# Mixing the running maxima and minima of two graph convolutions on ScalarE and VectorE instead of TensorE

## The chip, the cores and the metric

The kernel runs on one core of one Trainium2 chip. The metric is the device time of one execution in microseconds. TensorE multiplies, VectorE and ScalarE work elementwise, GpSimd issues the indirect DMAs (gathers and scatters by index), and SyncE issues most of the plain loads and fills. The engines run side by side, each through its own list of instructions in order, and wait for each other at semaphores.

## The reference

Eight graph layers run one after the other on the same 100,000 nodes of 128 features and 50,000 edges sorted by target: three GCN layers, two "eve" layers (`L1`), two SAGE layers and one attention layer. The change concerns the two eve layers alone. Cut to what matters, one of them is:

```
def eve_conv(x, src, dst, wpool, bpool, wself, weve, wconv, bconv, bias):
    p = relu(x @ wpool.T + bpool)
    m = p[src]
    xmax = segment_max(m, dst, num_segments=n)      # 0 where a node has no edge
    xmin = segment_min(m, dst, num_segments=n)
    eve = relu(wconv[0] * xmax + wconv[1] * xmin + bconv[0])
    return x @ wself.T + eve @ weve.T + bias

h = eve_conv(feat, ..., wpool1, ...); h = relu(h); h = eve_conv(h, ..., wpool2, ...)
x = layernorm(x + h)
```

`wconv` is two numbers and `bconv` one.

## The kernel before

Each layer is a phase of its own (`Conv`), called m4 and m5 for the two eve layers; a phase ends with a barrier of all engines. In a phase the edges are taken in 49 chunks of 1024 and the nodes in 49 pairs of chunks of 1024. On each engine `merged_sweep` writes the order: a unit of edge work (a pair of chunks, that is four halves of 512 edges), then the node pairs that the finished edges make ready (three each after the third and the fourth unit, two after each later one), then the next unit. There are 24 units of four halves and one of two, so 98 halves in a phase.

GpSimd (`pool_program`) has a list of its own: for each chunk eight gathers of 128 source rows into `rows` (L1073) and, four or five chunks behind, eight scatters of `result` into the table `sums` (L1081), with a copy of the indices (L1060) between. A scatter waits for `e_out_read`, which the last step of its half on VectorE raises.

A half `i` of the edge work (`EveEdges`) passes through these steps:

- TensorE turns the gathered rows into `e_turn` (L1122), of which there is one bank.
- ScalarE copies it to `xT` (L1486) and makes `begin` from the run flags (L1493).
- TensorE multiplies `xT` with the pooling weight into one of two banks named `pool` (L1435).
- ScalarE adds the bias and takes the relu in place (L1499).
- VectorE scans the bank twice, for the running maximum `hi` (L1531) and the running minimum `lo` (L1535).
- TensorE multiplies `hi` and `lo` with two diagonal matrices, the identity times `wconv[0]` and times `wconv[1]`, and sums both products into the same bank (L1442, L1443, function `mix`).
- ScalarE adds `bconv` and takes the relu into the SBUF tile `mix` (L1480).
- TensorE multiplies `mix` with `weve` into `e_out`, one bank (L1132).
- VectorE adds the bias into `result` (L1518).

On TensorE the order in half `i` is: mix of `i-1`, turn of `i+1`, multiply of `i-1`, pool of `i+1`. The mix and the product of a unit's last half therefore stand at the head of the next unit, behind the node pairs. The diagonal matrices (`k["mix1"]`, `k["mix2"]`) are made once in `load_constants` (L249).

The node work (`LinearNodes`) turns and multiplies a pair of node chunks on TensorE (L1190, L1208, in m5 also L1204 for a residual input), with `nodeT` on ScalarE (L1223), the sum `z` on VectorE (L1775) and the output `o` on ScalarE. In m4 this is one relu per chunk (L1811). In m5 it is a layer norm, with statistics on VectorE (L712), a root on ScalarE (L753) and sixteen scaled copies on ScalarE (L759).

Of the kernel before, what the change touches and what calls it, by code (L numbers as in the profile page):

```python
# [24 lines left out]
ALU = mybir.AluOpType  # L25
# [134 lines left out]
def load_constants(nc, a, k):  # L160
# [20 lines left out]
    with Phase(nc, "const") as ph:  # L181
# [14 lines left out]
        mix_made = ph.sem("mix_made")  # L196
# [8 lines left out]
        with nc.Block() as block:  # L205
# [38 lines left out]
            def _(dve):  # L244
                dve.wait_ge(loaded, 16 * len(loads))
                dve.wait_ge(ident_made, 1)
                for i in (1, 2):
                    for m in range(2):
                        dve.tensor_scalar(k[f"mix{i}"][:, m, :], k["ident"][:, :], k[f"wconv{i}"][:, m:m + 1], None, ALU.mult).then_inc(mix_made, 1)  # L249
                dve.wait_ge(mix_made, 4)  # L250
# [1156 lines left out]
class EveEdges:  # L1407


    def __init__(self, ph, no):  # L1410
# [3 lines left out]
        self.mix_w, self.bconv, self.bias = k[f"mix{no}"], k[f"bconv{no}"], k[f"eve_r{no}"]  # L1414
# [5 lines left out]
        self.mixed, self.mix_relu = ph.sem("mixed"), ph.sem("mix_relu")  # L1420
# [7 lines left out]
    def tensor(self, pe, j, par, q, halves, back):  # L1428
        ph = self.ph

        def pool(i):
            g = 4 * j + i
            pe.wait_ge(ph.e_turn_read, g + 1)
            wait_from(pe, self.mix_relu, g - 1)
            pe.matmul(self.bank[i % 2][:, :], self.wpool[:, :], self.xT[:, i % 2, :], start=True, stop=True).then_inc(self.pooled_ps, 1)  # L1435

        def mix(jj, i):

            g = 4 * jj + i
            pe.wait_ge(self.hi_done, g + 1)  # L1440
            pe.wait_ge(self.lo_done, g + 1)
            pe.matmul(self.bank[i % 2][:, :], self.mix_w[:, 0, :], self.hi[:, i % 2, :], start=True, stop=False)  # L1442
            pe.matmul(self.bank[i % 2][:, :], self.mix_w[:, 1, :], self.lo[:, i % 2, :], start=False, stop=True).then_inc(self.mixed, 1)  # L1443
# [14 lines left out]
        for i in range(halves):  # L1458
            before_half(mix, i)
# [9 lines left out]
        if halves == 0:  # L1469
            before_half(mix, 0)  # L1470
            before_half(multiply, 0)

    def scalar(self, act, j, par, q, halves, back):
        ph = self.ph

        def relu(jj, i):
            g = 4 * jj + i
            act.wait_ge(self.mixed, g + 1)
            wait_from(act, ph.e_multiplied, g - 3)
            act.activation(self.mix[:, i, :], self.bank[i % 2][:, :], ACT.Relu, bias=self.bconv[:, 0:1]).then_inc(self.mix_relu, 1)  # L1480
# [20 lines left out]
        for i in range(halves):  # L1501
# [5 lines left out]
            if i:  # L1507
                relu(j, i - 1)
        if halves == 0 and back:
            relu(j - 1, back - 1)  # L1510

    def vector(self, dve, j, par, q, halves, back):
# [13 lines left out]
        def scans(i):  # L1526
            g = 4 * j + i
            dve.wait_ge(self.pooled, g + 1)
            start = scan_start(dve, self.hi_done, self.hi, g, i)
            wait_from(dve, self.mixed, g - 1)  # L1530
# [6 lines left out]

        for i in range(halves):
            scans(i)
            result_before(i)  # L1540
# [1043 lines left out]
def build(nc, a, out):  # L2584
# [17 lines left out]
    with ExitStack() as ctx:  # L2602
# [29 lines left out]
        for n in ("mix1", "mix2"):  # L2632
            keep(n, [P, 2, D], stack=early)
# [46 lines left out]
```

## Time and profile before

| what | us |
|---|---|
| median of 3 runs (10847.68 to 10850.53) | 10850.13 |
| the profiled execution, its own time | 10843.73 |
| its span | 10841.9 |
| m4 (first eve layer), in the span | 4604 to 5627 |
| m5 (second eve layer) | 5627 to 6815 |

Busy shares over the whole span are 66% for GpSimd, 62% for TensorE, 57% for VectorE and 42% for ScalarE, but each layer has its own limit, so they are read by layer. In a view of stretches "PEclk" is the granted TensorE clock as a share of full speed. In a timeline a row gives the start, the duration, the engine, the line, what is written from what, and in brackets how long the engine had been idle and who released it. "issue" means that nothing the profile shows was waited for.

### The profile page before, as it was taken

What the parts mean: (1) busy time and instruction counts of PE and PEld (TensorE: products, weight loads), DVE (VectorE), ACT (ScalarE), POOL (GpSimd) and SP (SyncE); (2) the same over time, 40 slices, a digit from 0 to 9 for tenths busy, and PEclk for the clock granted to TensorE, in tenths of its full rate; (3) what the DMA queues carried; (4) which work ended last, traced back from release to release, by engine and by line L of the source; (5) the groups of instructions that cost most, each with busy time, mean ns of one, the idle gap of its engine ahead of it and who ended that gap; (6) DMA issues with size and microseconds to landing.
All of it is one profiled execution on the core that took longest, in us unless ns stands there. A gap on an engine that the chain in (4) does not pass through costs nothing. (4 is left out here: it accounts for less than half of the span.)

```text
span 10841.9 us, 165885 instructions
## 1 busy us (share of the span) xinstructions
PE 6744.0 (62%) x36946; PEld 5118.8 (47%) x36947; DVE 6202.3 (57%) x16059; ACT 4581.5 (42%) x8583; POOL 7208.8 (66%) x7532
## 2 busy tenths in 40 slices
PE   2005766677667669978767888445467656555552
PEld 2004666566656653355545555444455543333331
DVE  5225666566556656544435555333355547888888
ACT  0111222233223325544435555333345545777777
POOL 5736776777677750077767665677677767777772
PEclk9998888788889889988989999777778877777775
DMA  7887887799889978767768777677688863433333
GB/s 190 184 200 240 281 281 250 263 344 319 283 284 337 328 266 283 265 217 258 253 209 281 259 267 260 215 247 251 235 276 313 297 221 98 126 127 126 125 119 105
DMA packets 1864966, 2570.80 MB, mean 237 GB/s; under 512 B 255901, under 2 KB 1369141, under 8 KB 1864662
## 3 DMA queue, kind: packets, MB, share of 16 engines
q1 hardware_dynamic: 1134168, 1627.20, 45.5%
q10 hardware_dynamic: 504726, 564.87, 15.5%
q0 software_dynamic: 225792, 375.94, 10.9%
q14 instruction: 220, 1.80, 0.1%
q8 instruction: 60, 0.98, 0.0%
HBM read 1499.55 MB, written 1129.98 MB: 243 GB/s over the span
## 5 line engine op out<-in xcount | busy, mean ns | idle before, releaser
L1081 POOL DMA_INDIRECT sums_gcn<-m_result,m_idx x1176 | 1166.9, 992 | 430.9 <-issue 349.1
L1190 PE MATMUL m_n_bank<-k_ident,m_in_y 128*128 128x128 f32 x5488 | 848.1, 312 | 891.8 <-DMA m_in_y<-node_rows_c 381.0
L1073 POOL DMA_INDIRECT m_rows<-node_rows_a,m_idx x1176 | 1127.7, 959 | 339.6 <-issue 335.8
L1223 ACT ACTIVATE m_nodeT<-m_n_bank 128x512 f32<-128x512 f32 x980 | 535.6, 597 | 1725.7 <-PE m_n_bank L1190 1723.4
L1775 DVE TENSOR_TENSOR m_z<-m_n_bank,m_in_sums 128x512 f32<-128x512 f32 (+1 forms) x784 | 505.7, 686 | 1306.6 <-ACT m_o L1811 355.0
L1190 PEld LDWEIGHTS m_n_bank<-k_ident,m_in_y 128*128 128x128 f32 x5488 | 719.3, 162 | 983.7 <-issue 791.4
L1081 POOL DMA_INDIRECT sums_eve<-m_result,m_idx x784 | 766.0, 977 | 407.4 <-issue 230.1
L1081 POOL DMA_INDIRECT sums_sage<-m_result,m_idx x784 | 765.9, 977 | 268.4 <-issue 231.4
L1686 DVE SCALAR_TENSOR_TENSOR m_acc<-m_n_bank,m_scales,m_res_b 128x128 f32<-128x128 f32 (+1 forms) x2352 | 634.2, 342 | 487.7 <-PE m_n_bank L1208 421.0
L1073 POOL DMA_INDIRECT m_rows<-node_rows_b,m_idx x784 | 754.4, 962 | 226.4 <-issue 222.1
L1629 PE MATMUL m_gram<-m_y 128*128 128x129 f32 (+1 forms) x4800 | 689.5, 308 | 340.6 <-ACT m_y L1655 339.3
L1629 PEld LDWEIGHTS m_gram<-m_y 128*128 128x128 f32 (+1 forms) x4800 | 652.2, 220 | 374.8 <-ACT m_y L1655 372.9
L1122 PE MATMUL m_e_turn<-k_ident,m_rows 128*128 128x128 f32 x2744 | 512.0, 320 | 499.1 <-DVE m_sums L1585 183.6
L1122 PEld LDWEIGHTS m_e_turn<-k_ident,m_rows 128*128 128x128 f32 x2744 | 391.4, 166 | 637.5 <-DVE m_sums L1585 187.1
L759 ACT ACTIVATE m_o<-m_z,m_ln_shift,m_ln_scale 128x128 f32<-128x128 f32 x1600 | 628.4, 485 | 94.6 <-DMA node_rows_c<-m_o 45.0
L1060 POOL COPY m_idx<-k_edge_idx 128x16 int32 (+1 forms) x350 | 74.6, 215 | 872.5 <-POOLq L106 871.8
L2203 POOL DMA_INDIRECT sums_gat<-g_result,g_idx x392 | 453.3, 1156 | 294.3 <-DVE g_result L2497 179.7
L1208 PE MATMUL m_n_bank<-k_gcn,m_nodeT 128*128 128x128 f32 (+1 forms) x4704 | 589.6, 280 | 0.0
L1132 PE MATMUL m_e_out<-k_gcn,m_sums 128*128 128x128 f32 x2352 | 409.4, 329 | 286.7 <-DVE m_result L1402 286.7
L1931 POOL DMA_INDIRECT degree<-deg_both_tab,k_edge_idx x392 | 456.4, 1164 | 179.0 <-issue 119.2
L1208 PEld LDWEIGHTS m_n_bank<-k_gcn,m_nodeT 128*128 128x128 f32 (+1 forms) x4704 | 567.4, 197 | 0.0
L1132 PEld LDWEIGHTS m_e_out<-k_gcn,m_sums 128*128 128x128 f32 x2352 | 357.3, 232 | 346.4 <-DVE m_result L1402 180.9
(299 smaller groups left out, 17513.2 us busy)
## 6 DMA issues: line engine op xcount, KB each, us to landing
m_in_sums<-sums_gcn SPq DMA_DIRECT2D x291, 512.0 KB
m_in_y<-node_rows_a SPq DMA_DIRECT2D x291, 512.0 KB
sums_gcn<-k_gcn_b SPq DMA_DIRECT2D x194, 512.0 KB
node_rows_a<-m_y ACTq DMA_DIRECT2D x194, 512.0 KB
m_in_x<-in_x_dram SPq DMA_DIRECT2D x194, 512.0 KB
m_in_y<-node_rows_b SPq DMA_DIRECT2D x194, 512.0 KB
sums_eve<-k_eve_b SPq DMA_DIRECT2D x194, 512.0 KB
m_in_sums<-sums_eve SPq DMA_DIRECT2D x194, 512.0 KB
```

Of the source, the lines that this page charges most:

```text
L759: ins = act.activation(out[0:n, j, :], z[0:n, j, :], ACT.Identity, bias=self.shift[copy][0:n, at:at + 1], scale=self.scale[copy][0:n, at:a ...
L1073: pool.indirect_dma_start(self.rows[b][:, t, :], None, self.table[:, :], bass.IndirectOffsetOnAxis(self.idx[s][:, t:t + 1], 0)).then_inc(s ...
L1081: pool.indirect_dma_start(self.node_sums[:, :], bass.IndirectOffsetOnAxis(self.idx[s][:, T + t:T + t + 1], 0), self.result[b][:, t, :], No ...
L1122: mm = pe.transpose(bank[:, n * P:(n + 1) * P], self.rows[b][:, H * (i % 2) + n, 0:D], self.k["ident"][:, :])
L1132: mm = pe.matmul(bank[:, n * D:(n + 1) * D], lhs[:, n * P:(n + 1) * P], weight[:, :], start=True, stop=True)
L1190: mm = pe.transpose(self.n_bank[i][:, t * P:t * P + n], self.buf["y"][i // 2][0:n, H * (i % 2) + t, :], self.k["ident"][0:n, 0:n])
L1208: mm = pe.matmul(self.n_bank[i][0:n, t * D:(t + 1) * D], self.nodeT[:, i, t * P:t * P + n], weight[:, :], start=not add, stop=not add or t ...
L1223: act.activation(out, src, ACT.Copy).then_inc(self.n_turn_read, 1)
L1629: mm = pe.matmul(self.gram[:, 0:D + 1], self.y1[b][0:rows[b], t, 0:D], self.y1[b][0:rows[b], t, :], start=False, stop=False, skip_group_ch ...
L1686: ins = dve.scalar_tensor_tensor(out=self.acc[b][0:n, tt, :], in0=ph.node_out(i, n)[:, t, :], scalar=self.scales[b][0:n, tt:tt + 1], in1=s ...
L1775: dve.tensor_tensor(self.z[b][0:n, half, :], ph.node_out(i, n), ph.buf["sums"][b][0:n, half, :], ALU.add).then_inc(ph.n_out_read, 1)
L1931: pool.indirect_dma_start(self.dram["degree"][:, :], bass.IndirectOffsetOnAxis(k["edge_idx"][:, c, 1, t:t + 1], 0), self.both_tab[:, c * T ...
```

## The change

TensorE no longer mixes. After the scan of the maxima, ScalarE writes `wconv[0] * hi + bconv` into `mix` (new step `scale_hi`, an Identity with a scale and a bias). After the scan of the minima, VectorE adds `wconv[1] * lo` to it in place (new step `mix`, one instruction with `lo` and `mix`, both in SBUF, as inputs). ScalarE then takes the relu of `mix` in place. The diagonal matrices and the four instructions that made them are gone. The bank `pool` is free for the next product when the scan of the minima is done (`lo_done`), and no longer when the relu is. The line numbers of the change are lower than those of before by 5 to 9 here.

```
         def pool(i):
             pe.wait_ge(ph.e_turn_read, g + 1)
-            wait_from(pe, self.mix_relu, g - 1)
+            wait_from(pe, self.lo_done, g - 1)
             pe.matmul(self.bank[i % 2], self.wpool, self.xT[:, i % 2, :])
-        def mix(jj, i):
-            pe.wait_ge(self.hi_done, g + 1)
-            pe.wait_ge(self.lo_done, g + 1)
-            pe.matmul(self.bank[i % 2], self.mix_w[:, 0, :], self.hi[:, i % 2, :], start=True, stop=False)
-            pe.matmul(self.bank[i % 2], self.mix_w[:, 1, :], self.lo[:, i % 2, :], start=False, stop=True)
...
         def relu(jj, i):                                   # ScalarE
             act.wait_ge(self.mixed, g + 1)
-            wait_from(act, ph.e_multiplied, g - 3)
-            act.activation(self.mix[:, i, :], self.bank[i % 2], ACT.Relu, bias=self.bconv)
+            act.activation(self.mix[:, i, :], self.mix[:, i, :], ACT.Relu)
+        def scale_hi(i):
+            act.wait_ge(self.hi_done, g + 1)
+            wait_from(act, ph.e_multiplied, g - 3)
+            act.activation(self.mix[:, i, :], self.hi[:, i % 2, :], ACT.Identity, bias=self.bconv, scale=self.wconv[:, 0:1])
...
             pool(i)
             if i:
                 relu(j, i - 1)
+            scale_hi(i)
...
+        def mix(i):                                        # VectorE
+            dve.wait_ge(self.hi_scaled, g + 1)
+            dve.wait_ge(self.lo_done, g + 1)
+            dve.scalar_tensor_tensor(out=self.mix[:, i, :], in0=self.lo[:, i % 2, :], scalar=self.wconv[:, 1:2],
+                                     in1=self.mix[:, i, :], op0=ALU.mult, op1=ALU.add)
         for i in range(halves):
             scans(i)
+            mix(i)
             result_before(i)
```

ScalarE in the third half of a unit, before (the first row is the relu of an earlier half, the others are the copy, `begin` and the pooling relu of the next one):

```order
L1480 ACTIVATE m_mix<-m_pool,k_bconv 128x512
L1484 REGISTER_ALU
L1486 ACTIVATE m_xT<-m_e_turn 128x512
L1493 REGISTER_ALU
L1493 ACTIVATE m_begin<-k_same_run 128x512
L1499 ACTIVATE m_pool<-m_pool,k_bpool 128x512
```

And at the same place in the change:

```order
L1464 ACTIVATE m_mix<-m_mix 128x512
L994 REGISTER_ALU
L1470 ACTIVATE m_mix<-m_hi,k_bconv,k_wconv 128x512
L1475 REGISTER_ALU
L1477 ACTIVATE m_xT<-m_e_turn 128x512
L1484 REGISTER_ALU
L1484 ACTIVATE m_begin<-k_same_run 128x512
L1490 ACTIVATE m_pool<-m_pool,k_bpool 128x512
```

The scaling of `hi` now stands between the relu and the copy of the next half.

VectorE in the same half, before:

```order
L1531 SCALAR_TENSOR_TENSOR m_hi<-k_same_run,m_hi,m_pool 128x512
L1535 SCALAR_TENSOR_TENSOR m_lo<-m_begin,m_lo,m_pool 128x512
L1518 TENSOR_TENSOR m_result<-m_e_out,k_eve_r 128x512
L1528 REGISTER_ALU
L1531 REGISTER_ALU
```

And in the change:

```order
L1524 SCALAR_TENSOR_TENSOR m_hi<-k_same_run,m_hi,m_pool 128x512
L1528 SCALAR_TENSOR_TENSOR m_lo<-m_begin,m_lo,m_pool 128x512
L1535 SCALAR_TENSOR_TENSOR m_mix<-m_lo,k_wconv,m_mix 128x512
L1510 TENSOR_TENSOR m_result<-m_e_out,k_eve_r 128x512
L1520 REGISTER_ALU
L1524 REGISTER_ALU
```

The addition stands behind the two scans and ahead of the previous half's result. (The first two rows are the scans; the trace names them TENSOR_TENSOR_SCAN.)

## Rows read from the trace of the kernel before

**Rows 1.** Stretches: start:end, length, busy us of each engine, PEclk, DMA share.

```profile
core 0: us, PE busy (x) PEld busy (x) DVE busy (x) ACT busy (x) POOL busy (x), PEclk, DMA share, GB/s
4604.00:5627.00 1023.00, 772.21 (x4116) 543.01 (x4116) 431.59 (x492) 439.11 (x688) 766.79 (x834) 0.90 0.73 243
5627.00:6815.00 1188.00, 935.87 (x4508) 605.94 (x4508) 646.79 (x1627) 659.65 (x1438) 766.83 (x834) 0.92 0.74 252
...
5720.00:6740.00 1020.00, 833.40 (x4040) 542.82 (x4040) 573.25 (x1469) 585.67 (x1281) 680.43 (x737) 0.93 0.78 270
6950.00:7700.00 750.00, 375.88 (x2719) 360.94 (x2720) 267.85 (x541) 258.91 (x304) 575.64 (x625) 0.76 0.74 260
7900.00:8800.00 900.00, 632.85 (x3573) 509.54 (x3574) 513.73 (x1669) 513.88 (x1042) 690.49 (x749) 0.82 0.87 306
```

**Rows 2.** Waits of GpSimd in m4, then in m5: total us, times, longest.

```profile
POOL sums_eve L1081 <- DVE m_result L1518: 7.2, 1, 7.2
...
POOL sums_eve L1081 <- DVE m_result L1518: 167.7, 22, 23.8
```

**Rows 3.** Groups by line, 5720 to 6740: busy us, mean ns, idle before.

```profile
L1442 PE MATMUL m_pool<-m_hi,k_mix 128*128 128x512 f32 x170 | 97.5, 658 | 14.7 <-DVE m_lo L1535 14.7
L1443 PE MATMUL m_pool<-m_lo,k_mix 128*128 128x512 f32 x170 | 90.0, 612 | 0.0
```

**Rows 4.** Timeline of one unit of m5, three engines.

```profile
5861.71 1.28 DVE L1531 TENSOR_TENSOR_SCAN m_hi<-k_same_run,m_hi,m_pool 128x512 f32<-128x512 f32 x1 [1.67 <-ACT m_pool L1499]
...
5864.66 1.27 DVE L1531 TENSOR_TENSOR_SCAN m_hi<-k_same_run,m_hi,m_pool 128x512 f32<-128x512 f32 x1
...
5869.96 1.28 DVE L1531 TENSOR_TENSOR_SCAN m_hi<-k_same_run,m_hi,m_pool 128x512 f32<-128x512 f32 x1 [0.95 <-ACT m_pool L1499]
...
5871.56 0.59 ACT L1486 ACTIVATE m_xT<-m_e_turn 128x512 f32<-128x512 f32 x1
5871.72 1.16 PE L1132 MATMUL m_e_out<-k_eve,m_mix 128*128 128x128 f32 x8 [0.42 <-ACT m_mix L1480]
5872.04 0.63 ACT L1493 ACTIVATE m_begin<-k_same_run 128x512 f32 x1
5872.71 1.02 PE L1435 MATMUL m_pool<-m_xT,k_pool 128*128 128x512 f32 x2
5873.57 1.02 PE L1442 MATMUL m_pool<-m_hi,k_mix 128*128 128x512 f32 x2
5873.77 0.66 ACT L1499 ACTIVATE m_pool<-m_pool,k_bpool 128x512 f32<-128x512 f32 x1 [1.10 <-PE m_pool L1435]
5874.43 1.02 PE L1443 MATMUL m_pool<-m_lo,k_mix 128*128 128x512 f32 x2
5874.56 1.28 DVE L1531 TENSOR_TENSOR_SCAN m_hi<-k_same_run,m_hi,m_pool 128x512 f32<-128x512 f32 x1 [0.95 <-ACT m_pool L1499]
5876.23 1.16 PE L1132 MATMUL m_e_out<-k_eve,m_mix 128*128 128x128 f32 x8 [0.78 <-ACT m_mix L1480]
```

**Rows 5.** The attention layer's timeline, VectorE and GpSimd; then two groups of the page.

```profile
9068.14 0.75 DVE L2476 SCALAR_TENSOR_TENSOR g_prob<-g_val,k_blb,g_prob 128x512 f32<-128x512 f32 x1
9068.93 1.28 DVE L2479 TENSOR_TENSOR_SCAN g_num<-g_fall,g_num,g_prob 128x512 f32<-128x512 f32 x1
...
9069.19 1.80 POOL L2203 DMA_INDIRECT sums_gat<-g_result,g_idx  x1 [0.30 <-issue]
...
L1081 POOL DMA_INDIRECT sums_eve<-m_result,m_idx x784 | 766.0, 977 | 407.4 <-issue 230.1
...
L2203 POOL DMA_INDIRECT sums_gat<-g_result,g_idx x392 | 453.3, 1156 | 294.3 <-DVE g_result L2497 179.7
```

**Rows 6.** Timeline of m5 from node work into the next unit.

```profile
5899.13 1.02 PE L1443 MATMUL m_pool<-m_lo,k_mix 128*128 128x512 f32 x2
...
5903.23 0.69 ACT L1480 ACTIVATE m_mix<-m_pool,k_bconv 128x512 f32<-128x512 f32 x1 [2.22 <-issue]
...
5905.76 1.91 PE L1435 MATMUL m_pool<-m_xT,k_pool 128*128 128x512 f32 x2
```

**Rows 7.** Timeline of VectorE in the constants phase.

```profile
32.57 0.87 DVE L249 TENSOR_SCALAR k_mix<-k_ident,k_wconv 128x128 f32<-128x128 f32 x4 [32.45 <-DMA k_bconv<-in_L_gnn_bconv_dram]
```

More of the change, by code:

```diff
@@ L246, in _ @@
                 dve.wait_ge(ident_made, 1)
[L247 to L250, printed above, removed]
                 for i, n in enumerate(turned):
@@ L1413, in __init__ @@
         self.wpool, self.weve, self.bpool = k[f"pool{no}"], k[f"eve{no}"], k[f"bpool{no}"]
-        self.mix_w, self.bconv, self.bias = k[f"mix{no}"], k[f"bconv{no}"], k[f"eve_r{no}"]
+        self.wconv, self.bconv, self.bias = k[f"wconv{no}"], k[f"bconv{no}"], k[f"eve_r{no}"]
         self.xT, self.begin, self.hi, self.lo = (ph.sb(n, [P, 2, HALF]) for n in ("xT", "begin", "hi", "lo"))
@@ L1419, in __init__ @@
         self.hi_done, self.lo_done = ph.sem("hi_done"), ph.sem("lo_done")
-        self.mixed, self.mix_relu = ph.sem("mixed"), ph.sem("mix_relu")
+        self.hi_scaled, self.mixed, self.mix_relu = ph.sem("hi_scaled"), ph.sem("mixed"), ph.sem("mix_relu")
     def sync(self, sp, j, par, q, halves, back):
@@ L1458, in tensor @@
         for i in range(halves):
-            before_half(mix, i)
             if i + 1 < halves and i:
@@ L1469, in tensor @@
         if halves == 0:
-            before_half(mix, 0)
             before_half(multiply, 0)
@@ L1478, in relu @@
             act.wait_ge(self.mixed, g + 1)
+            act.activation(self.mix[:, i, :], self.mix[:, i, :], ACT.Relu).then_inc(self.mix_relu, 1)
+        def scale_hi(i):
+            g = 4 * j + i
+            act.wait_ge(self.hi_done, g + 1)
             wait_from(act, ph.e_multiplied, g - 3)
-            act.activation(self.mix[:, i, :], self.bank[i % 2][:, :], ACT.Relu, bias=self.bconv[:, 0:1]).then_inc(self.mix_relu, 1)
+            act.activation(self.mix[:, i, :], self.hi[:, i % 2, :], ACT.Identity, bias=self.bconv[:, 0:1],
+                           scale=self.wconv[:, 0:1]).then_inc(self.hi_scaled, 1)
         def copy(i):
@@ L1529, in scans @@
             start = scan_start(dve, self.hi_done, self.hi, g, i)
+            wait_from(dve, self.hi_scaled, g - 1)
             wait_from(dve, self.mixed, g - 1)
@@ L1536, in scans @@
                                    ALU.min).then_inc(self.lo_done, 1)
+        def mix(i):
+            g = 4 * j + i
+            dve.wait_ge(self.hi_scaled, g + 1)
+            dve.wait_ge(self.lo_done, g + 1)
+            dve.scalar_tensor_tensor(out=self.mix[:, i, :], in0=self.lo[:, i % 2, :], scalar=self.wconv[:, 1:2], in1=self.mix[:, i, :],
+                                     op0=ALU.mult, op1=ALU.add).then_inc(self.mixed, 1)
         for i in range(halves):
             scans(i)
+            mix(i)
             result_before(i)
```

6 lines of the change are left out of this document (removed).

## The prediction

> **What bounds the kernel now.** I read the stretches of the two layers first, then who waits for whom, then one unit row by row. In m4 (4604 to 5627) GpSimd is busy 767 of 1023 us [rows 1], and the rest is almost all the fixed gap between its indirect DMAs: it waits for a result only once, 7.2 us, at the very end [rows 2]. An indirect DMA takes 0.977 us and the gap 0.30 [rows 5], so 49 chunks of 16 make 784 x 1.277 = 1001 us. The reader should see that m4 is GpSimd's issue time and nothing else: whatever TensorE saves there ends nothing sooner. In m5 GpSimd has the same 784 to issue, but the layer takes 1188 us, and it waits 167.7 us for `m_result` in 22 waits [rows 2]. There the units and the node pairs, in their fixed order on TensorE, ScalarE and VectorE, set the pace, with TensorE busy 833 of 1020 us [rows 1]. A gain can come from m5 alone, and at most about those 167.7 us.
>
> **TensorE's removed work, and what is late next.** The two removed products hold TensorE from 5873.57 to about 5875.29, that is 1.72 us a half at the full clock [rows 4], 187.5 us in the 1020 us of m5 [rows 3]. In the regular rhythm before, starts of the scan of the maxima stand 4.60 us apart (5869.96, 5874.56) [rows 4], and TensorE fills that time with one idle gap of 0.42. After the change the rhythm is another chain, since ScalarE's list has the new scaling behind the scan and ahead of the next copy: scan 1.28 plus 0.05 to ScalarE, scaling until the copy can start 0.55 (not in the trace; the nearest rows are 0.63 for `m_begin` from SBUF and 0.59 for the copy, which overlap their follower by about 0.1), copy 0.59 and 0.05, pooling product until ScalarE starts 1.06 (5872.71 to 5873.77), its relu 0.66 and 0.13 to the scan (5873.77 to 5874.56) [rows 4]. The sum is 4.37 us. VectorE itself needs at most 2 x 1.28 for the scans and 2 x 0.75 for the addition and the result, 4.1 us a half, so it isn't the bound. The first gap of a unit was 2.95 (5861.71 to 5864.66) and the second 5.30 [rows 4]; all three now become 4.37. Three gaps make 13.1 instead of 12.85: **0.25 us lost per unit**. At a unit's end TensorE was done with the product of the third half at 5876.23 + 1.16, or 2.83 after the last scan's start [rows 4]; now the relu of that half needs no mix, starts right behind the pooling relu (5874.43), takes 0.63, and the product ends about 1.65 after the scan's start. The nodes' first turn follows TensorE, so the node pairs start 1.18 us sooner. Net 0.93 us x 24 units = **-22 us in m5**, at the full clock. What must hide there: ScalarE's last scaling ends about 2.0 after the scan's start, before the first turned nodes reach it.
>
> At a unit's start nothing is gained. TensorE had the last half's mix done by 5900.15, but ScalarE, still with the nodes' outputs, came to its relu at 5903.23 [rows 6]. The mix was already hidden, and the same relu is late in the change.
>
> **The clock.** In the 1020 us of m5 TensorE was granted 0.93. Where it is less busy it is granted less: 0.82 at 70% busy and 0.76 at 50% [rows 1]. Without the 187.5 us it would be 63% busy in m5, so I take 0.82. With two levels, 2.4 and 1.2 GHz, the low one holds for 14% of the time before and 36% after. At the low level the pooling product, which is on the new chain, runs 1.91 instead of 1.02 at 5905.76 [rows 6, 4], and ScalarE starts about 1.0 later. 98 halves x 0.22 x 1.0 = **+22 us in m5**. The bounds are 0 (the clock holds) and 45 (a low share of 60% in the edge work). In m4 the same is covered by GpSimd, as long as a pair of units' chain stays under its 41 us a unit.
>
> **The addition and GpSimd.** The new addition reads two tensors in SBUF. No VectorE step of the edge work did so before. What that does is to be seen in the attention layer: a scan with two SBUF inputs runs 1.28 us from 9068.93, to 9070.21, and the scatter that GpSimd began at 9069.19 takes 1.80 us instead of 0.97, ending 0.78 after the scan [rows 5]. Its fixed part behind the hold is thus about 0.77, and the hold lasts from 0.2 after its start to the scan's end. Over that layer a scatter takes 1156 ns against 977 in the eve layers [rows 5]. For an instruction of length L that falls anywhere in GpSimd's rhythm of 1.277, the expected hold is L x L / (2 x 1.277). The addition is not in the trace; the nearest row is the 0.75 of L2476 [rows 5], which gives 0.22 us, and 0.69 would give 0.19. 98 x 0.20 = **+20 us in m4**, where GpSimd is the bound and every hold counts. The bounds are 0 (it never meets) and 98 x 0.5 = 49 (it always meets in the middle). In m5 GpSimd has its waits to swallow it; I take **+5**, between 0 and 20.
>
> The Trainium skill, page "SBUF — State Buffer", section "Who interferes with whom", says that a VectorE instruction with two SBUF inputs contends with a GpSimd instruction that reads SBUF, and that the second to start is blocked for the whole of the first. By that rule the change has this price. The trace agrees, with 1.80 against 0.97 us [rows 5]. The same section of the Trainium skill infers that `tensor_tensor` doesn't hold up descriptor generation, since that needs the write side. By that the price would be nil and the sum 25 us lower, and the row of 1.80 us speaks against it.
>
> **The rest.** The four multiplications for the diagonal matrices, 0.87 us with their wait [rows 7], go; the first weights were turned 0.4 us later than these began, so about **-1**. ScalarE's scaling costs 98 x 0.55 = 54 us of its time per layer; it is in the chain above for m5, and in m4 (439 us busy of 1023 [rows 1]) it is covered. The wait for `hi_scaled` on VectorE ends during the scan of the minima (about 1.28 us, like the other, against 0.05 + 0.63). Behind ScalarE's new wait for `hi_done` stand the copy, `begin` and the pooling relu of the next half, and TensorE and VectorE wait for those: that is the chain counted above.
>
> **The sum.** m4 +20; m5 -22 + 22 + 5 = +5; constants -1; together +24. From the profiled execution's 10843.7 that is 10867.7; the median of the runs stands 6.4 above it, so **10874 us**.
>
> **Rivals.**
> - The clock holds: m5's +22 is nil and the time 10852. For it: the units' regular part keeps TensorE 60% busy in short gaps only. Against: 0.82 at 70% [rows 1].
> - The clock is low in most of the edge work: +45 (98 x 0.46 x 1.0) instead of +22, so 10897. For it: at a unit's start it is low already, and there is less work than before to raise it [rows 6].
> - GpSimd is not held: 25 less, 10849. Against it stands the 1.80 [rows 5].
> - Faster: ScalarE comes to the first relu of a unit sooner than now. If it gains the 3.1 us by which it is late behind TensorE's mix [rows 6], the removed mix at a unit's head counts too: 24 x 1.72 = 41 us more, and GpSimd's waits in m5 shrink with it. Then the time is 10874 - 41 - 5 = 10828 or less. It decides when ScalarE's relu starts within 0.1 us of its mix being there. Against it: ScalarE gets more work, not less.
> - The change doing nothing at all isn't open: the products are gone from TensorE's list.
>
> **How the numbers follow.** The forecast has 0.43, and its own range is 10859 to 10889; the low clock 0.24, the held clock 0.14, GpSimd not held 0.08, faster 0.11. A measurement of this kernel tells about 0.2%, 22 us, from no change, so the limits are 10828 and 10872. The forecast lies on the upper one and gives 0.23 to slower and 0.20 to same; with the low clock slower has 0.47; the held clock, GpSimd not held and 0.01 of the last rival bring same to 0.43; faster has 0.10. The range from 10835 to 10905 leaves out the faster rival and what lies above the low clock's.
>
> **What would show it.** Right: m4 longer by 16 to 24 us, with indirect DMAs of 1.1 to 1.6 us wherever the addition runs, and a mean over all of m4 up by 0.02 to 0.03; m5 within 15 us of its 1188; granted clock near 0.82 in m5; scan starts 4.3 to 4.5 apart at the full clock. Wrong: m4 unchanged (GpSimd isn't held), m5 shorter by over 20 (the clock or the unit's start), or scan starts under 4.2 apart.

## The result, and the profile after

The change makes the kernel slower. Its median is 10903.74 us (10893.25 to 10909.83) against 10847.68 us of the kernel before in the same measurement; the ratio is 1.0055 with a 95% interval of 1.0042 to 1.0069. The forecast was +24 us and it came to +56: above the forecast's own range (10859 to 10889), and only just inside the wide one (up to 10905). The profiled execution has a span of 10905.8 us against 10841.9.

I measure a layer from its first indirect DMA to the first one of the next layer, since GpSimd's list is the same in both kernels.

| stretch | before | after | difference | forecast |
|---|---|---|---|---|
| up to m4's first DMA | 4605.2 | 4603.1 | -2.1 | -1 |
| m4 | 1023.6 | 1038.8 | +15.2 | +20 |
| m5 | 1187.8 | 1242.8 | +55.0 | +5 |
| from m6 to the end | 4025.3 | 4021.0 | -4.3 | 0 |

So m4 came out near what was worked out, and the error is in m5. The stretches of m4, of m5 and of the steady part of m5, in the change (start:end, length, busy us of each engine with instruction counts, PEclk, DMA share, GB/s; compare [rows 1]):

```profile
4603.00:5641.00 1038.00, 669.71 (x3724) 528.07 (x3724) 500.98 (x590) 506.88 (x786) 781.40 (x832) 0.80 0.73 240
5641.00:6884.00 1243.00, 850.10 (x4116) 599.32 (x4116) 715.58 (x1726) 728.92 (x1536) 780.10 (x837) 0.82 0.71 241
5720.00:6790.00 1070.00, 756.36 (x3702) 535.14 (x3702) 630.44 (x1534) 645.97 (x1365) 703.27 (x750) 0.84 0.74 255
```

TensorE lost its 392 mix records in each layer, yet its busy time in m5 fell by only 86 us (935.87 before, 850.10 now), since what is left ran slower: the granted clock fell from 0.92 to 0.82. In m4 GpSimd's busy time rose from 766.79 to 781.40, with the same DMAs.

GpSimd's waits in m4 and then in m5 of the change (us in total, times, longest; compare [rows 2]):

```profile
POOL sums_eve L1076 <- DVE m_result L1510: 8.5, 1, 8.5
...
POOL sums_eve L1076 <- DVE m_result L1510: 208.7, 21, 25.3
```

In m4 it still waits once, at the end. In m5 its waits grew by 41 us; the DMAs themselves are 13 us longer (below), and that is the 54 by which the time from its first to its last DMA grew (1159.0 to 1213.4). m5 is paced by the other engines, as forecast.

**The regular chain.** Two halves of m5 in the change at the full clock (start, duration, engine, line; compare [rows 4]):

```profile
6038.34 1.28 DVE L1524 TENSOR_TENSOR_SCAN m_hi<-k_same_run,m_hi,m_pool 128x512 f32<-128x512 f32 x1 [0.77 <-ACT m_pool L1490]
...
6039.66 0.81 ACT L1470 ACTIVATE m_mix<-m_hi,k_bconv,k_wconv 128x512 f32<-128x512 f32 x1 [0.89 <-DVE m_hi L1524]
...
6040.38 0.58 ACT L1477 ACTIVATE m_xT<-m_e_turn 128x512 f32<-128x512 f32 x1
...
6040.90 0.75 DVE L1535 SCALAR_TENSOR_TENSOR m_mix<-m_lo,k_wconv,m_mix 128x512 f32<-128x512 f32 x1
...
6041.01 1.13 PE L1430 MATMUL m_pool<-m_xT,k_pool 128*128 128x512 f32 x2 [1.03 <-ACT m_xT L1477]
6041.19 1.30 POOL L1076 DMA_INDIRECT sums_eve<-m_result,m_idx  x1 [0.30 <-issue]
...
6042.17 0.66 ACT L1490 ACTIVATE m_pool<-m_pool,k_bpool 128x512 f32<-128x512 f32 x1 [0.70 <-PE m_pool L1430]
...
6042.95 1.28 DVE L1524 TENSOR_TENSOR_SCAN m_hi<-k_same_run,m_hi,m_pool 128x512 f32<-128x512 f32 x1 [0.71 <-ACT m_pool L1490]
```

The chain is the one of the prediction, scan, scaling, copy, product, relu, scan, but 4.61 us long and not 4.37: the copy starts 0.72 behind the scaling and not 0.55, and ScalarE's relu 1.16 behind the product's start and not 1.06, because TensorE now comes to the product from an idle gap (in the kernel before, the product at 5862.06 came from one of 0.83, and there it was 1.17). The row at 6041.19 is a held DMA, one that took longer than its usual 0.97 because VectorE's addition was running: it began 0.29 after the addition's start and took 1.30 instead of 0.97.

**The first gap of a unit.** The same chain where the clock is low:

```profile
6075.69 1.28 DVE L1524 TENSOR_TENSOR_SCAN m_hi<-k_same_run,m_hi,m_pool 128x512 f32<-128x512 f32 x1 [3.39 <-ACT m_pool L1490]
...
6077.08 0.81 ACT L1470 ACTIVATE m_mix<-m_hi,k_bconv,k_wconv 128x512 f32<-128x512 f32 x1 [1.68 <-DVE m_hi L1524]
6077.80 0.58 ACT L1477 ACTIVATE m_xT<-m_e_turn 128x512 f32<-128x512 f32 x1
...
6078.43 2.07 PE L1430 MATMUL m_pool<-m_xT,k_pool 128*128 128x512 f32 x2 [2.87 <-ACT m_xT L1477]
...
6080.54 0.66 ACT L1490 ACTIVATE m_pool<-m_pool,k_bpool 128x512 f32<-128x512 f32 x1 [1.64 <-PE m_pool L1430]
...
6081.32 1.28 DVE L1524 TENSOR_TENSOR_SCAN m_hi<-k_same_run,m_hi,m_pool 128x512 f32<-128x512 f32 x1 [1.72 <-ACT m_pool L1490]
```

TensorE had been idle for 2.87 us and the product takes 2.07 instead of 1.13. Scan to scan is 5.63 us. Of 21 units the three gaps averaged 3.14, 5.67 and 4.59 before and average 5.40, 5.00 and 4.68 now, 15.08 in sum instead of 13.40. From a unit's last scan to the next unit's first one it was 33.87 and is 34.45.

**The end of a unit.** The nodes' first turn, in the kernel before and in the change (TensorE alone):

```profile
6347.10 1.96 PE L1190 MATMUL m_n_bank<-k_ident,m_in_y 128*128 128x128 f32 x16 [0.71 <-issue]
6393.07 1.96 PE L1190 MATMUL m_n_bank<-k_ident,m_in_y 128*128 128x128 f32 x16 [0.83 <-issue]
...
6240.34 3.50 PE L1185 MATMUL m_n_bank<-k_ident,m_in_y 128*128 128x128 f32 x16 [0.82 <-issue]
6387.12 3.50 PE L1185 MATMUL m_n_bank<-k_ident,m_in_y 128*128 128x128 f32 x16 [0.71 <-issue]
```

Between 5870 and 6700 us this turn ran at the full clock, in 1.96 us, at all 18 unit ends before, and in the change at 5 of the 17 whose turn stands in one row; at the other 12 it took 2.43 to 3.51. ScalarE waits for it, and the node pairs behind it. This is the loss that the prediction has no term for.

### The profile page after: what moved, and what is told of

The parts are those of the page before. It is cut to its first block and busy times, and to the rows that moved or that the text cites. A ratio compares the mean times of both kernels' runs of the same rounds, so it can differ in the third digit from the quotient of the medians.

```text
span 10905.8 us, 164896 instructions
## 1 busy us (share of the span) xinstructions
PE 6525.5 (60%) x36162; PEld 5068.9 (46%) x36163; DVE 6332.6 (58%) x16251; ACT 4716.2 (43%) x8779; POOL 7234.6 (66%) x7532
## 5 line engine op out<-in xcount | busy, mean ns | idle before, releaser
L1185 PE MATMUL m_n_bank<-k_ident,m_in_y 128*128 128x128 f32 x5488 | 878.2, 320 | 880.6 <-DMA m_in_y<-node_rows_c 386.2
L1185 PEld LDWEIGHTS m_n_bank<-k_ident,m_in_y 128*128 128x128 f32 x5488 | 748.4, 166 | 973.2 <-issue 771.4
L1117 PE MATMUL m_e_turn<-k_ident,m_rows 128*128 128x128 f32 x2744 | 536.2, 331 | 498.3 <-DVE m_sums L1586 173.5
L1127 PE MATMUL m_e_out<-k_eve,m_mix 128*128 128x128 f32 x1568 | 308.4, 357 | 353.8 <-ACT m_mix L1464 349.3
```

Of the source, the lines that this page charges most:

```text
L1117: mm = pe.transpose(bank[:, n * P:(n + 1) * P], self.rows[b][:, H * (i % 2) + n, 0:D], self.k["ident"][:, :])
L1127: mm = pe.matmul(bank[:, n * D:(n + 1) * D], lhs[:, n * P:(n + 1) * P], weight[:, :], start=True, stop=True)
L1185: mm = pe.transpose(self.n_bank[i][:, t * P:t * P + n], self.buf["y"][i // 2][0:n, H * (i % 2) + t, :], self.k["ident"][0:n, 0:n])
```

## The experiments

Two theories of m5's 55 us. A: ScalarE's order, with the scaling between a scan and the next copy, makes most of it. B: the lower clock makes most of it. A third matter is whether the two SBUF inputs of the addition hold GpSimd. The table has all runs; the ratio is to the kernel before, measured on the same chip, "held" counts the DMAs of a layer that took over 1.05 us. The layer columns come from one profiled execution of each kernel, whose total can stand far from the kernel's median (10898.61 against 10877.00 for extra_add, 10878.77 against 10862.30 for product_and_psum, 10807.53 against 10826.82 for no_scale). What the two layers differ by from before agrees with the difference of the medians within 15 us in each kernel, so differences of 10 us between rows are weak evidence by themselves.

| kernel | ratio (95%) | m4 | m5 | clock m5 | held m4, m5 |
|---|---|---|---|---|---|
| before | 1 | 1023.6 | 1187.8 | 0.92 | 0, 0 |
| change | 1.0055 (1.0042 to 1.0069) | 1038.8 | 1242.8 | 0.82 | 37, 40 |
| only_m5 | 1.0039 (1.0025 to 1.0053) | 1021.9 | 1238.0 | 0.83 | 0, 38 |
| psum_input | 1.0035 (1.0021 to 1.0049) | 1031.1 | 1232.9 | 0.83 | 0, 0 |
| extra_add | 1.0016 (1.0007 to 1.0025) | 1037.5 | 1205.2 | 0.90 | 27, 18 |
| no_scale | 0.9987 (0.9978 to 0.9996) | 1024.1 | 1167.1 | 0.86 | 7, 3 |
| late_scale | 0.9968 (0.9956 to 0.9980) | 1022.8 | 1151.4 | 0.87 | 9, 3 |
| late_first | 1.0029 (1.0019 to 1.0040) | 1030.4 | 1210.0 | 0.82 | 34, 27 |
| late_filler | 1.0008 (0.9999 to 1.0017) | 1032.6 | 1190.7 | 0.85 | 45, 17 |
| extra_product | 1.0019 (1.0010 to 1.0028) | 1035.9 | 1199.7 | 0.90 | 35, 26 |
| product_and_psum | 1.0011 (1.0002 to 1.0020) | 1018.7 | 1208.6 | 0.88 | 0, 0 |
| extra_scale | 1.0088 (1.0075 to 1.0102) | 1056.2 | 1267.8 | 0.89 | 0, 0 |
| late_product | 0.9954 (0.9940 to 0.9968) | 1021.6 | 1130.8 | 0.90 | 6, 4 |

**One layer alone.**

> The change in the second eve layer alone, m4 as before. The two layers don't touch each other: m4 1022 to 1024, m5 1244 as in the change, total 10885 to 10892. If m5 comes out shorter than 1235, part of its loss was carried over from m4 (the state of the clock at its start, or the chip).

It went as expected: m4 as before, m5 within 5 us of the change's. The layers are independent, and 5 us is also how far two profiles of the same m5 stood apart here.

**The addition's inputs.**

```
-            wait_from(pe, self.lo_done, g - 1)
+            wait_from(pe, self.mixed, g - 1)
...
-            dve.scalar_tensor_tensor(out=self.mix[:, i, :], in0=self.lo[:, i % 2, :], ...
+            dve.scalar_tensor_tensor(out=self.mix[:, i, :], in0=self.bank[i % 2][:, :], ...
```

> The addition reads the PSUM bank in place of lo, so that it has one SBUF input (mix) instead of two; the minima are left out of the result. Theory (two SBUF inputs hold GpSimd's indirect DMAs): m4 goes back from 1038 to 1023 to 1026, the mean scatter in it from 996 to about 977 ns, and m5 gains 0 to 5 us; total 10883 to 10890. Rival (m4's 15 us come from the added steps' timing, not from their inputs): m4 stays at 1036 to 1040 and the total at 10900.

GpSimd's groups in m5, first of the change, then of this kernel (busy us, mean ns):

```profile
L1076 POOL DMA_INDIRECT sums_eve<-m_result,m_idx x392 | 389.9, 995 | 322.2 <-DVE m_result L1510 208.7 <-issue 112.6 <-DMA sums_eve<-m_result,m_idx 0.9
L1068 POOL DMA_INDIRECT m_rows<-node_rows_a,m_idx x392 | 379.4, 968 | 113.2 <-issue 112.9 <-PE m_e_turn L1117 0.3
...
L1076 POOL DMA_INDIRECT sums_eve<-m_result,m_idx x392 | 382.5, 976 | 326.5 <-DVE m_result L1510 213.6 <-issue 112.3 <-DMA sums_eve<-m_result,m_idx 0.6
L1068 POOL DMA_INDIRECT m_rows<-node_rows_a,m_idx x392 | 372.8, 951 | 113.1 <-issue 113.1
```

The addition takes as long (751 ns), and with one input in PSUM not one DMA is held. The mechanism is shown. In m4 the DMAs are 14 us shorter in sum (769.4 to 755.1), but only 7.7 of the 15 us came back, so the number expected of m4 was missed. GpSimd's last wait shows why:

```profile
POOL sums_eve L1076 <- DVE m_result L1510: 17.6, 2, 14.7
```

It was 8.5. Behind GpSimd the slowed units of m4 stand close, and took half of what it got back. m5 gained 10.

**The same addition in the kernel before**, its result discarded:

```
             scans(i)
+            dve.wait_ge(self.lo_done, 4 * j + i + 1)
+            dve.scalar_tensor_tensor(out=self.extra, in0=self.lo[:, i % 2, :], scalar=self.wconv[:, 1:2], in1=self.hi[:, i % 2, :],
+                                     op0=ALU.mult, op1=ALU.add)
             result_before(i)
```

> The kernel before, with the same addition of two SBUF tensors on VectorE (0.75 us a half, its result discarded) behind the two scans, in both layers. VectorE has room for it. Theory (a GpSimd DMA that starts inside such an addition is held): 25 to 45 DMAs of each layer take over 1.05 us, none in the kernel before; GpSimd's DMA time in each layer is 8 to 20 us longer; m4 is 5 to 18 us longer and m5 0 to 15 us; the ratio to before 1.001 to 1.003. Rival (the held DMAs come with ScalarE's scaling): no DMA over 1.05 us and no change.

It holds DMAs and brings m4's 14 us with no other part of the change, and 17 in m5, slightly over the bound that I set there. The rival, that ScalarE's scaling holds the DMAs, falls. The 14 and the 17 are not all holds: the DMA time grew by 9.1 us in m4 and 5.7 in m5, the step also lengthens VectorE's list (a unit's first gap is 3.76 instead of 3.14), and this profile is 22 us above its kernel's median. The cleaner figure for m5 is the 10 us of the kernel with one input in PSUM, where the DMA time fell by 14; the forecast had 5.

**The scaling taken away, and the scaling placed late.** In the first kernel:

```
-            act.activation(self.mix[:, i, :], self.mix[:, i, :], ACT.Relu)
+            act.activation(self.mix[:, i, :], self.mix[:, i, :], ACT.Relu, bias=self.bconv, scale=self.wconv[:, 0:1])
...
-            scale_hi(i)
...
-            dve.scalar_tensor_tensor(..., in0=self.lo[:, i % 2, :], scalar=self.wconv[:, 1:2], in1=self.mix[:, i, :], ...
+            dve.scalar_tensor_tensor(..., in0=self.lo[:, i % 2, :], scalar=self.ratio, in1=self.hi[:, i % 2, :], ...
```

> The scaling is gone from ScalarE: the addition is now hi + (w1/w0) * lo, and the relu applies w0 and the bias (w1/w0 is made once among the constants). ScalarE's next copy no longer stands behind the scan of the maxima. Theory A (the scaling between scan and copy made the chain of m5): scan starts in a unit come 4.0 to 4.4 apart at all three gaps, 12.0 to 13.2 instead of 15.1 for three, so 24 units are 45 to 75 us shorter; m5 from 1244 to 1170 to 1200, m4 stays at 1038 because the two-input addition is still there. Total 10830 to 10860. Theory B (the low TensorE clock made m5 longer, whatever the order on ScalarE): m5 stays over 1220 and the total over 10880.

In the second:

```
             copy(i)
             begin(i)
+            if i:
+                scale_hi(i - 1)
             pool(i)
             if i:
                 relu(j, i - 1)
-            scale_hi(i)
+        if halves:
+            scale_hi(halves - 1)
```

> Only the place of the scaling in ScalarE's list is changed: the copy and begin of the next half go ahead of it, and the scaling is still 0.8 us long. Theory A (its place between scan and next copy is what costs): m5 shortens like in the kernel without scaling, by 40 to 70 us, to 1175 to 1205, with scan starts 4.1 to 4.5 apart, the first gap of a unit included; m4 stays at 1038; total 10835 to 10865. Rival (ScalarE's added work itself costs, wherever it stands): m5 shortens by under 20 us, while the kernel without scaling gains more.

Both beat the kernel before. m5 is 76 and 91 us shorter than in the change, more than expected, and m4 lost its 15 us too, which I had not expected. Theory B as it stood here (m5 over 1220 whatever the order) falls, and so does the rival: with the same work in another order the whole loss is gone. The granted clock rose as well, from 0.82 to 0.86 and 0.87, so this is not the order at an unchanged clock. VectorE in the second kernel:

```profile
4968.36 1.28 DVE L1527 TENSOR_TENSOR_SCAN m_hi<-k_same_run,m_hi,m_pool 128x512 f32<-128x512 f32 x1 [0.74 <-ACT m_pool L1490]
...
4969.56 1.25 DVE L1531 TENSOR_TENSOR_SCAN m_lo<-m_begin,m_lo,m_pool 128x512 f32<-128x512 f32 x1
...
4970.92 0.75 DVE L1538 SCALAR_TENSOR_TENSOR m_mix<-m_lo,k_wconv,m_mix 128x512 f32<-128x512 f32 x1
...
4971.59 0.68 DVE L1513 TENSOR_TENSOR m_result<-m_e_out,k_eve_r 128x512 f32<-128x512 f32 x1
...
4972.19 1.27 DVE L1527 TENSOR_TENSOR_SCAN m_hi<-k_same_run,m_hi,m_pool 128x512 f32<-128x512 f32 x1
```

It has no idle gap of more than 0.11 us left between two scans of the maxima, 3.83 us apart; the gaps of a unit are 3.84, 3.92 and 3.82 (3.85, 3.95, 4.01 without the scaling). The work on ScalarE is the same as in the change, 0.81 us a half. What costs is its place. That the kernel without scaling is 16 us longer in m5 than the one with it stays open; its relu carries the scale and the bias, and I didn't take it apart.

**The first scaling alone.**

```
             copy(i)
             begin(i)
+            if i == 1:
+                scale_hi(0)
             pool(i)
             if i:
                 relu(j, i - 1)
-            scale_hi(i)
+            if i:
+                scale_hi(i)
```

> The change, with only the first half's scaling of each unit moved behind the copy and begin of the second half; the other three stay where the change has them. Theory A: the first gap goes from 5.40 back to 3.8 to 4.3 and the others stay at 4.7 to 5.0, so m5 is 24 x 1.1 to 24 x 1.6 = 26 to 38 us shorter (1205 to 1217) and the total 10866 to 10880. Theory B (the order matters only as a whole, since the next gap takes up what the first one gives): the three gaps still sum to 14.5 or more and m5 shortens by under 15 us.

m5 is 33 us shorter, as theory A has it. But the gaps are 3.83, 5.42 and 5.12: the first is repaired, and part of it is lost in the next ones, 14.37 in sum. That is 17 us over 24 units; the rest is in the stretch from a unit's last scan to the next first one, 33.84 instead of 34.45. The granted clock is 0.82, as in the change. So neither theory is whole.

**The clock.**

```
             before_half(multiply, i)
+            if 0 < i and i + 1 < halves:
+                pe.matmul(self.bank[(i + 1) % 2][:, 0:HALF // 2], self.wpool, self.mix[:, i - 1, 0:HALF // 2])
             if i == 0:
                 pool(0)
                 if halves > 1:
                     ph.turn_half(pe, j, par, q, 1, ph.e_turn_read)
+                    pe.matmul(self.bank[1], self.wpool, self.xT[:, 0, :])
```

> The change, with discarded products on TensorE where it waits in a unit (one of 512 columns before the second pooling product, where it is idle for 2.95 us on the mean, and one of 256 before the third and fourth, idle for 0.55 and 1.02). They only keep TensorE busy. Theory A (ScalarE's order makes most of m5's 55 us, the lower clock 10 to 30): the granted clock of m5 rises from 0.83 to 0.87 to 0.92 and m5 shortens by 5 to 30 us, to 1213 to 1238; the first gap stays above 4.6. Theory B (the clock makes it nearly all): m5 comes within 15 us of before's 1188. If the products themselves are in the way, m5 is longer than 1243.

m5 shortens by 43 us, to within 12 of the kernel before. That is theory B's number, from work that computes nothing; the first gap, 4.96 on the mean, stayed above 4.6, as theory A had it. Its stretches of m4 and m5, and then the pooling product's group in m5 in the change and here:

```profile
4621.00:5657.00 1036.00, 678.51 (x3870) 530.52 (x3870) 502.47 (x591) 505.70 (x786) 781.30 (x834) 0.85 0.72 240
5657.00:6856.00 1199.00, 837.32 (x4262) 580.87 (x4262) 715.88 (x1725) 726.65 (x1536) 772.64 (x834) 0.90 0.73 250
...
L1430 PE MATMUL m_pool<-m_xT,k_pool 128*128 128x512 f32 x196 | 158.0, 900 | 112.1 <-ACT m_xT L1477 112.0
...
L1430 PE MATMUL m_pool<-m_xT,k_pool 128*128 128x512 f32 x196 | 132.0, 761 | 78.9 <-ACT m_xT L1480 78.6
```

With more to do TensorE is busy for less time (850.10 to 837.32). The gaps sum to 14.25 instead of 15.08, and from a unit's last scan to the next first one it takes 33.39 instead of 34.45: more than half of the gain lies in the node pairs, whose first turn takes 1.96 us at 12 of 17 unit ends now, instead of 5. m4, bound by GpSimd and its held DMAs, moved by 3.

**Both repairs.**

> The change with both repairs: the discarded products that keep TensorE's clock up, and the addition reading the PSUM bank instead of lo (the minima are left out of the result). If the clock (43 us of m5's 54 between GpSimd's first and last DMA) and the held DMAs (10) are all of the loss and add up, m5's DMAs span 1157 to 1166 us, as in the kernel before (1159), m4's 1004 to 1012, and the ratio to before is 0.999 to 1.001. If the scaling in ScalarE's chain costs something of its own, m5's span stays at 1170 or more.

(The edits are those of the two kernels above.) m4 is undone in full, 1018.7, and a little more. m5 is not: 1208.6 against 1187.8, at a clock of 0.88 against 0.92. Its DMAs span 1179 us, on the side of the rival (1170 or more). So the two don't add up to all of m5's loss: 21 us are left by the profile, and the medians of the whole kernels are 12 apart. The gaps, 14.12 in sum instead of 13.40, account for 0.7 x 24 = 17 us; how much of that is the longer chain and how much the clock still missing isn't separated.

**The scaling in the kernel before**, result discarded, at the change's place:

```
             if i:
                 relu(j, i - 1)
+            act.wait_ge(self.hi_done, 4 * j + i + 1)
+            act.activation(self.extra, self.hi[:, i % 2, :], ACT.Identity, bias=self.bconv, scale=self.wconv[:, 0:1]).then_inc(self.extra_done, 1)
...
             start = scan_start(dve, self.hi_done, self.hi, g, i)      # VectorE, scans(i)
+            wait_from(dve, self.extra_done, g - 1)
```

> The kernel before with the scaling of hi on ScalarE at the same place of its list, its result discarded. TensorE still mixes, so its clock stays near 0.93 in m5. It shows the price of the longer chain without the clock. By the chain of the change (scan 1.28, scaling 0.72 until the copy, copy 0.64, product 1.16, relu 0.79) all three gaps come near 4.6, 13.8 to 14.1 in sum instead of 13.4, and m5 is 8 to 25 us longer; m4 within 4 us; no DMA over 1.05 us. If m5 is unchanged within 5 us, the place of the scaling costs nothing as long as TensorE's mix sets the gap.

This missed by far: 33 us in m4 and 80 in m5, at a clock of 0.89. The second gap of one of its units:

```profile
6072.60 1.28 DVE L1538 TENSOR_TENSOR_SCAN m_hi<-k_same_run,m_hi,m_pool 128x512 f32<-128x512 f32 x1 [1.58 <-ACT m_pool L1502]
6072.95 1.91 PE L1446 MATMUL m_pool<-m_lo,k_mix 128*128 128x512 f32 x2
...
6074.97 0.69 ACT L1483 ACTIVATE m_mix<-m_pool,k_bconv 128x512 f32<-128x512 f32 x1 [2.50 <-PE m_pool L1446]
6075.56 0.80 ACT L1513 ACTIVATE m_extra<-m_hi,k_bconv,k_wconv 128x512 f32<-128x512 f32 x1
...
6078.85 1.28 DVE L1538 TENSOR_TENSOR_SCAN m_hi<-k_same_run,m_hi,m_pool 128x512 f32<-128x512 f32 x1 [1.15 <-ACT m_pool L1502]
```

The same relu in the kernel before, at the same gap of a unit:

```profile
5866.38 0.69 ACT L1480 ACTIVATE m_mix<-m_pool,k_bconv 128x512 f32<-128x512 f32 x1 [2.49 <-PE m_pool L1443]
```

ScalarE's relu waited for TensorE's mix before too, 2.49 us against 2.50, and the next copy stood behind it in both. What is new is the scaling between them, 0.70 us from its start to the copy's, and a mix that is done later: the relu starts 2.37 us after the scan instead of 1.72. The gap is 6.25 instead of 5.30. More of the loss lies in the first gap, where no relu stands ahead of the copy and only the scaling makes it wait for the scan: 5.42 on the mean instead of 3.14, as in the change. All three are 5.42, 6.17 and 4.88, 16.47 in sum instead of 13.40, or 74 of m5's 80 us.

The four kernels together show where the low clock of the first gap comes from. The second pooling product of each of the 25 units in m5:

| kernel | mix on TensorE | scaling on ScalarE | idle before it, mean us | over 1.5 us, of 25 |
|---|---|---|---|---|
| before | yes | none | 0.76 | 8 |
| change | no | ahead of the copy | 2.95 | 20 |
| extra_scale | yes | ahead of the copy | 2.94 | 22 |
| late_scale | no | behind the copy | 0.74 | 2 |

At the full clock it takes 1.12, at the low one 2.07. (The unit shown above is one of extra_scale's three with a fast one.) So this product is slow where the scaling's place leaves TensorE idle ahead of it, whether TensorE mixes or not; taking the mix away doesn't slow it by itself.

The change is thus two large parts against each other: the scaling at this place costs 0.9% while TensorE mixes, and all the rest of the change, the mix removed and the addition put in, gives back less than half of that.

**Two rhythms.** m4's 15 us had gone in the kernel with the late scaling, though its addition has two SBUF inputs as well. There VectorE's rhythm of 3.83 us is three times GpSimd's 1.277. To put it off this ratio, a discarded half result:

```
             dve.wait_ge(ph.e_multiplied, 4 * jj + i + 1)
+            dve.tensor_tensor(self.extra, ph.edge_out(i)[:, 0:2, :], spread_slots(self.bias[:, :], [P, 2, D]), ALU.add)
             ph.result_free(dve, p, n, i)
```

> The kernel with the scaling placed late, plus a discarded VectorE step of half a result (0.35 us, one input in PSUM) per half. With the scaling late the scans start 3.82 us apart, which is three times GpSimd's rhythm of 1.277, and only 9 DMAs of m4 were held, where the change with 4.6 to 5.0 apart had 37. Theory A (two rhythms of a whole ratio settle where they don't meet): with 4.15 to 4.25 us apart (3.3 rhythms) 20 to 45 DMAs of m4 are held again and its DMA time rises by 6 to 15 us. Theory B (the scaling's place itself keeps the DMAs free): fewer than 15 held. In both m5 is 24 x 3 x 0.37 = 20 to 35 us longer, since VectorE is the bound of a unit there.

45 DMAs of m4 are held again instead of 9, and its DMA time rises by 9.6 us (758.0 to 767.6). GpSimd's groups in m4, with the late scaling alone and with the filler:

```profile
L1076 POOL DMA_INDIRECT sums_eve<-m_result,m_idx x392 | 383.8, 979 | 124.7 <-issue 115.8 <-DVE m_result L1513 5.5 <-DMA sums_eve<-m_result,m_idx 3.0
...
L1076 POOL DMA_INDIRECT sums_eve<-m_result,m_idx x392 | 387.4, 988 | 124.9 <-issue 115.1 <-DVE m_result L1515 5.8 <-DMA sums_eve<-m_result,m_idx 4.0
```

Theory A of that run holds: a held DMA shifts GpSimd until the two no longer meet, and with a whole ratio they stay so. Two other traces bear it out within one kernel. In m4 of late_first only the second addition of a unit comes 3.78 to 3.88 us after the one before; of these 24 one held a DMA, of the 50 that follow at another distance within a unit 24 did. In late_scale, where almost all follow at that distance, it was 1 of 62, and 7 of its 9 holds are at a unit's first addition. m5 was 39 us longer, slightly over the 35.

**The late scaling with a busier TensorE.**

```
+            if i:
+                pe.wait_ge(self.hi_done, 4 * j + i)
+                n = HALF if i + 1 == halves else HALF // 2
+                pe.matmul(ph.n_bank[0][:, 0:n], self.wpool, gat_e[:, 0:n])
             before_half(multiply, i)
...
                     ph.turn_half(pe, j, par, q, 1, ph.e_turn_read)
+                    pe.matmul(self.bank[1][:, 0:HALF // 2], self.wpool, self.xT[:, 0, 0:HALF // 2])
```

> The kernel with the scaling placed late, plus discarded products in TensorE's idle time (256 columns before the second pooling product; in each later half 256, in the last 512, before the product with weve, into a bank of the nodes). If the low clock of the node pairs still costs there as in the change, the granted clock of m5 rises from 0.87 to over 0.91 and m5 shortens by 5 to 25 us; total 10790 to 10805 against 10810. If the products are in the way, or the clock doesn't matter once VectorE is the bound of a unit, m5 is unchanged or longer.

Stretches of m4 and m5 with the late scaling alone, and then with the products:

```profile
4605.00:5628.00 1023.00, 634.39 (x3724) 525.71 (x3724) 497.54 (x591) 512.68 (x786) 768.97 (x834) 0.82 0.70 243
5628.00:6779.00 1151.00, 787.14 (x4116) 569.03 (x4116) 708.83 (x1725) 733.55 (x1536) 766.54 (x834) 0.87 0.76 261
...
4625.00:5647.00 1022.00, 646.53 (x3920) 518.98 (x3920) 496.23 (x591) 508.77 (x786) 767.30 (x834) 0.85 0.71 243
5647.00:6777.00 1130.00, 818.44 (x4312) 580.19 (x4312) 708.94 (x1725) 731.07 (x1536) 765.89 (x834) 0.90 0.77 265
```

m5 is another 21 us shorter. The gaps, bound by VectorE, hardly moved (11.57 to 11.48 in sum); the stretch between units went from 33.78 to 32.94, with the first turn at 1.96 us at 17 of 19 unit ends instead of 7. With the units' gaps unchanged, this is what the clock is worth outside their chain, about 20 us by the profiles. The ratios to the kernel before, 0.9968 and 0.9954, are 15 us apart, and their intervals overlap, so the gain in the whole time isn't secure. It is the lowest median of the study, 10800.74 us against 10810.06 with the late scaling alone.

## Why the prediction was right or wrong

- **m4 is GpSimd's, +20: right in its mechanism, a little high.** +15.2, just under the 16 to 24 named as its sign, with the DMA time up by 12.9 us (756.5 to 769.4), 0.016 a DMA and not 0.02 to 0.03. The hold, taken as 0.20 an addition, came to 12.9 / 98 = 0.13: a DMA counted as held where it began 0.1 to 0.55 us into the addition, and ended about 1.58 after the addition's start (0.11 + 1.47, 0.36 + 1.23, 0.47 + 1.10). Of the 196 additions of both layers 77 held one. The "Who interferes with whom" section of the page "SBUF — State Buffer" of the Trainium skill says that a VectorE instruction with at most one SBUF input (outside its two-port modes) doesn't contend with GpSimd, and that one with two contends with a GpSimd instruction that reads SBUF. By that rule the holds go with one input moved to PSUM, and the trace agrees, 37 against 0 in m4. The same section of the Trainium skill infers that a `tensor_tensor` doesn't hold descriptor generation, because its second input takes only the read side. The addition here is a `scalar_tensor_tensor`, so that isn't tested as it stands, but 27 DMAs held in m4 by a discarded addition with two SBUF inputs speak against the reason.
- **m5 as a whole, +5: wrong.** Per unit the three gaps grew by 1.68 us (13.40 to 15.08) and the stretch from the last scan to the next first one by 0.58 (33.87 to 34.45); 24 times their sum is 54 us. The forecast had 0.25 and -1.18 for the two at the full clock, and 4 x 0.22 for the clock.
- **m5's chain at the full clock, -22: wrong, the first failed step.** The regular chain was the right one, and two of its terms were off by 0.17 and 0.10, so the gap is 4.61 and not 4.37. Over three gaps and 24 units that is 17 us. The gain at a unit's end, 1.18 us, was priced from TensorE's being done sooner; where the clock was best kept (extra_product), the stretch from a unit's last scan to the next first one was 0.48 shorter than before. There the whole period of a unit is 47.61 us against 47.29, 0.32 x 24, so all of this comes to about +8, 26 held DMAs and a clock of 0.90 instead of 0.92 included, instead of -22.
- **The clock, +22: the largest failed step.** The forecast of the granted clock was near (0.82; it is 0.82 over all of m5 and 0.84 in its steady part), in part by luck. The mean says nothing of where in a unit the low clock falls, and the 187.5 us of removed work count the overlap of the two products twice; without their rows the other products cover 155 us less of the 1020, which leaves TensorE 66% busy and not 63%, and it came out 71% busy because what was left ran slower. The price was not near. I charged it to one product in the chain, 98 x 0.22 x 1.0. Raising the clock from 0.82 to 0.90 gave back 43 us, and more than half of that in the stretch with the node pairs, which the prediction left out: the first turn behind a unit, 1.96 us before and 2.43 to 3.51 at most unit ends now, stands on ScalarE's way to the nodes. Within a unit the low clock sits where the chain is most exposed to it, in the first gap (5.63 with the product at 2.07), which was 2.95 before, since the scaling was not ahead of the copy then. A mean share of low time was the wrong measure for both.
- **Order and clock are not two separate sums.** Placing the scaling late gave back 91 us with the clock at 0.87, the discarded products 43 with the order kept, and the loss was 55. In the first gap the low clock is itself the work of the order: the second product is slow in 20 units of 25 with the scaling ahead of the copy, in 22 with the mix kept as well, and in 2 with the scaling late. What each would cost with the other held fixed isn't measured.
- **The constants, -1:** m4 starts 2.1 us earlier; other profiles of this study start it up to 28 us later (4633.6), so this can't be read.
- **Contention in m5, +5: too small.** One input in PSUM gave back 10. The 17 of the discarded addition contain more than the holds, and a profile of the same m5 repeats within about 5.
- **The sum.** +8 and +43 make 51 of m5's 55; the other 4 lie outside the units counted. The rival of the low clock, 10897, came nearest, and its argument, that the clock is low at a unit's start already, is what the rows show. That its number is near is luck all the same: its 45 was worked out from the products of the units alone, without the node pairs, and stood beside a -22 that didn't come.
- **The faster rival** didn't occur: from the start of the nodes' last sum to the next unit's first scan it takes 6.73 us on the mean against 6.29 (medians 6.65 and 6.62), so nothing came sooner there.
- **"VectorE itself needs 4.1 us a half, so it isn't the bound"** was right for the change and named the floor of the better order; measured it is 3.82, because the result takes 0.68 and not 0.75 and consecutive steps overlap by up to 0.1 us.

## What to carry to other kernels

Work taken off TensorE can have a price. Here its granted clock fell from 0.92 to 0.82 and its pooling product took up to 2.07 us instead of 1.13, while the steps of ScalarE and VectorE kept their durations (0.66 and 1.28). Look for the steps of TensorE on others' paths behind the place that is thinned out, and price them at their low-clock duration. When a new step has to go into an engine's list, put it behind what starts the next round; the same scaling on ScalarE stands in a kernel 0.6% slower and, moved behind the next copy, in one 0.3% faster than before. Keep one input of a VectorE step in PSUM where GpSimd's indirect DMAs set the pace. And where a loop of VectorE runs against GpSimd's rhythm, the holds can't be forecast from a mean overlap alone.

## What the runs showed of the hardware

- A DMA that GpSimd issues is held by a VectorE instruction with two SBUF inputs if it begins between about 0.1 and 0.53 us into it (all 77 of the change), and then it ends 1.57 to 1.63 after the instruction's start. The upper edge comes from counting only DMAs over 1.05 us as held. The other way round nothing is held: 125 of the 196 additions of the change began while a DMA's issue was running, and took 0.751 us on the mean, against 0.754 for the others.
- In m4 the holds depend on the ratio of the two rhythms. At 3.83 us against 1.277, a ratio of three, 9 of m4's DMAs were held; at about 4.2 us 45; at 4.6 to 5.3 us 37.
- Products that compute nothing made the kernel faster: 43 us in m5 of the change, and 21 us where the scaling was late, with the granted clock at 0.90 in both instead of 0.82 and 0.87.
- The place of one ScalarE step decided at which clock TensorE's next product ran: 2 of 25 second products were slow with the scaling behind the copy, 20 with it ahead, with the same 4116 TensorE instructions in m5 in both.
